# Matmuls of weight zero moved from every tile of keys to seven tiles around each change of heads

## The reference

```python
qh = (q @ Wq.T + bq).reshape(b, t, h, d).transpose(0, 2, 1, 3)
kh = (k @ Wk.T + bk).reshape(b, -1, h, d).transpose(0, 2, 1, 3)
attn = jax.nn.softmax(jnp.einsum('bhtd,bhsd->bhts', qh, kh) * scale, axis=-1)
out = jnp.einsum('bhts,bhsd->bhtd', attn, vh)
...
x = x + jnp.tanh(g_xattn[0]) * _L0_xattn_ref(_layernorm(x, axis=-1), ctx_1024, ctx_1024, ...)
x = x + jnp.tanh(g_ffn[0]) * _L0_ffn_ref(_layernorm(x, axis=-1), ...)
x = x + jnp.tanh(g_xattn[1]) * _L1_xattn_ref(ctx_1024, ctx_1024, _layernorm(x, axis=-1), mask_Bx1xSxS2_bf1, ...)
x = x + jnp.tanh(g_ffn[1]) * _L1_ffn_ref(_layernorm(x, axis=-1), ...)
```

## Time and profile before

| | |
|---|---|
| median of 3 runs | 2881.51 us (2869.57 to 2913.2) |
| the profiled execution: time, span, mean granted clock | 2875.57 us, 2873.5 us, 0.927 |
| PE busy | 2664.2 us, 93% |
| DVE busy | 2173.8 us, 76% |
| ACT busy | 1946.9 us, 68% |
| chain that ended last | PE 88%, of that L967 32%, L919 25%, L938 14%, L986 6% of the span |

### The profile page before, as it was taken

How to read it: one execution, slowest core, us unless ns; L and a number is a source line. 1 busy time by engine, 2 the same in 40 slices (tenths; PEclk the granted TensorE clock), 3 DMA queues, 4 the chain that set the end, 5 groups by cost and what they waited for, 6 DMA issues and landing times.

```text
span 2873.5 us, 63043 instructions
## 1 busy us (share of the span) xinstructions
PE 2664.2 (93%) x27154; PEld 1107.1 (39%) x27156; DVE 2173.8 (76%) x2210; ACT 1946.9 (68%) x3545; POOL 41.2 (1%) x28
## 2 busy tenths in 40 slices
PE   2489999999999999999693899999999999999989
PEld 1244344444444433344341344444444443444444
DVE  5478788888888877863533888888888887888334
ACT  1158778878888877786330288887888886888842
POOL 3000000000000000000001000000000000000000
PEclk8569899999999988999895699999999998999989
DMA  6210000000000000002201000000000000000010
GB/s 239 80 58 28 22 26 27 28 27 28 28 26 26 26 26 21 24 15 92 91 1 55 13 28 28 28 27 26 26 27 27 28 28 22 27 26 19 2 60 8
DMA packets 38657, 103.60 MB, mean 36 GB/s; under 512 B 4164, under 2 KB 14936, under 8 KB 38120
## 3 DMA queue, kind: packets, MB, share of 16 engines
q1 hardware_dynamic: 36936, 99.14, 9.4%
q10 hardware_dynamic: 1440, 0.40, 0.1%
HBM read 83.72 MB, written 15.80 MB: 35 GB/s over the span
## 4 chain that ended last, share of the span: by engine, by line
PE 88%; DVE 5%; DMA 3%; SPq 3%; ACT 1%; issue 1%; POOL 0%; ACTq 0%; DVEq 0%; POOLq 0%
PE ps L967 32%; PE ps L919 25%; PE ps L938 14%; PE ps L986 6%; PE ps L1065 3%; DVE m_part L650 3%; PE ps L1073 3%; SPq L290 2%; PE ps L879 1%; DMA q_parts<-probs 1%; SPq L299 1%; PE ps L909 1%; DMA probs<-in_mask_t 1%; DVE probs L606 1%; DMA k_parts<-probs 1%
## 5 line engine op out<-in xcount | busy, mean ns | idle before, releaser
L650 DVE TENSOR_REDUCE m_part<-ps 128x2 f32<-128x1024 f32 (+1 forms) x1664 | 1946.2, 1184 | 346.6 <-PE ps L938 239.8
L488 ACT ACTIVATE probs<-ps 128x512 f32<-128x512 f32 (+1 forms) x3264 | 1771.0, 595 | 482.7 <-PE ps L919 468.3
L967 PE MATMUL ps<-probs,v_all 128*9 128x256 f32 x13056 | 1033.5, 389 | 1.4 <-ACT o_raw L468 0.5
L919 PE MATMUL ps<-q_ring,k_ring 35*128 35x512 f32 x3264 | 852.0, 506 | 0.4
L938 PE MATMUL ps<-k_ring,q_ring 33*128 33x512 f32 (+1 forms) x3328 | 718.2, 425 | 90.4 <-DVE m_part L650 36.2
L919 PEld LDWEIGHTS ps<-q_ring,k_ring 35*128 35x128 f32 x3264 | 328.4, 186 | 554.9 <-ACT probs L488 500.2
L986 PE MATMUL ps<-neg_i,zeros 128*9 128x256 bf16 x6392 | 475.4, 277 | 0.0
L967 PEld LDWEIGHTS ps<-probs,v_all 128*9 128x9 f32 x13056 | 194.4, 88 | 564.4 <-ACT probs L488 455.2
L938 PEld LDWEIGHTS ps<-k_ring,q_ring 33*128 33x128 f32 x3328 | 336.6, 197 | 179.5 <-DVE m_part L650 104.6
L986 PEld LDWEIGHTS ps<-neg_i,zeros 128*9 128x9 bf16 x6392 | 175.1, 89 | 176.4 <-issue 14.3
L671 DVE RECIPROCAL r_den<-ps 128x8 f32<-128x8 f32 x32 | 6.6, 207 | 123.4 <-PE ps L946 123.4
(11 more groups left out here) (121 smaller groups left out, 601.2 us busy)
## 6 DMA issues: line engine op xcount, KB each, us to landing
k_ring<-k_parts SPq DMA_DIRECT2D x384, 96.0 KB
k_ring<-k_parts SPq DMA_DIRECT2D x128, 112.2 KB
k_ring<-gate_rows SPq DMA_DIRECT2D x16, 512.0 KB, 7.0
probs<-in_mask_t SPq DMA_DIRECT2D x10, 640.0 KB, 4.4
k_parts<-probs SPq DMA_DIRECT2D x12, 512.0 KB, 3.1
k_parts<-big SPq DMA_DIRECT2D x12, 512.0 KB, 3.1
q_ring<-q_parts SPq DMA_DIRECT2D x128, 32.0 KB
big<-in_w SPq DMA_DIRECT2D x1, 2048.0 KB, 11.3
```

What stands on the lines that cost most here:

```text
L488: A(probs[0:k, n % PSLOTS, HALF * half:HALF * half + HALF], ps[0:k, e_bank(unit), :], ACT.Exp, scale=SCALE).then_inc(sem(f"exp_done{l}"), 1)
L650: V.tensor_reduce(m_part[:, h % 2, :, p, c], mx(n % 2)[:, :, 0:chunk_w[c]], AX.X, ALU.max).then_inc(sem(f"mx_done{l}"), 1)
L919: pe.matmul(bank, k_ring[row:row + ROWS_EXP, koff:koff + P], q_ring[row:row + ROWS_EXP, qoff:qoff + HALF], start=not masked, stop=True).th ...
L967: mm = pe.matmul(ps[32 * g:32 * g + VW, 7, 0:QGW], v_all[0:k, t, h, :], probs[0:k, n % PSLOTS, QGW * g:QGW * g + QGW], start=(t == 0), sto ...
```

## The change

The loop that issues groups now issues three of them in a row after the weighing of tiles 0, 1, 2, 3, 47, 48 and 49 of a head (NT is 51), and none after any other tile. Weighing runs two steps behind, so these are steps 2 to 5 of a head, its steps 49 and 50, and step 0 of the next. Nothing else changes. Executed groups go from 50 a head to 21 (the last head of a layer: 49 to 18), recorded matmuls of L986 from 6392 to 2664. In the changed kernel's listing all PE lines are 4 higher.

```diff
@@ -60,6 +60,10 @@
 EB = 3
 LAG = 2
 WARM = 5
+
+
+DENSE = 3
+DENSE_AT = (0, 1, 2, 3, NT - 4, NT - 3, NT - 2)
 
 
 KCH = -(-TK // HALF)
@@ -1012,7 +1016,7 @@
                         n = h * NT + t - LAG
                         if n >= 0:
                             weigh(l, n // NT, n % NT)
-                            if n % NT < NT - 1:
+                            for _ in range(DENSE if n % NT in DENSE_AT else 0):
                                 keep_warm()
```

## The result

The changed kernel takes 2749.14 us (median of 3 runs, 2748.89 to 2751.86) against 2881.51 before: a ratio of 0.9563, 95% interval 0.9514 to 0.9612. Forecast was 2744 us. The profiled execution took 2751.86 us, its span is 2749.9 us. The spread of three runs went from 44 us to 3 us. In the changed kernel's listing the lines of PE are 4 higher than before: score L923, max L942, weigh L971, group L990.

The account below looks back on a forecast made before the run. PE was taken to set the pace in mid-head, partly at half clock. From 2875.6 us, 82 for fewer groups and 49 for the clock come off, giving 2744 us; own range 2727 to 2765, 2705 to 2800 for 0.8.

Parts of the forecast that it names:

- Part one: Saving from removed groups, net of added ones: 2.6 us a head over 30 heads, some 3 us from two last heads.
- the six falls: Six heads of the earlier profile partly at half clock, losing 48.8 us together; all six taken as gone.
- Its two terms: Per head: 43 middle tiles save 0.096 us each, 4.1 us; 14 added groups cost 0.107 each, 1.5 us.
- PE sets the pace there too, so I hide none of it: At the seven tiles with three groups, every added group costs its full 0.107 us, 1.5 us a head.
- my 1.33: Mean time in us from score to score in a head before the change, taken as 67.7/51.
- The score banks' loop: A score's first half to next tile's second half takes at least 1.24 us, making middle tiles 1.23, not 1.22.
- Part two: Clock gain at heads' ends: three groups where one stood keep the clock up, giving 49 us.
- the thin stretch at a head's end: PE's last work in a head, few rows: two max units, a 35-row score, a 4-row weighing; the clock falls behind it.
- my 131: Total forecast saving in us, the 82 from groups and the 49 from the clock.
- The middle falls: Rival: without groups the clock falls in the middle of heads, 880 us more, about 3620 us; chance 0.08.
- Another wait in place of the groups: Rival: another wait keeps middle tiles at 1.33 us, so 2872 us; chance 0.05.
- Falls that remain and last: Rival: three groups don't hold the clock at heads' ends; six falls cost 38 us each, 2972 us; chance 0.06.

Follow-up runs that it names:

- experiment 1: Changed kernel with one group put back after every other tile except a head's last, the three at the seven tiles kept: 2869.85 us, ratio 0.9979 to the kernel before.
- Experiment 6: Changed kernel with exponentials of 448 instead of 512 columns after each layer's first head: 2727.51 us, median of six; a head falls from 67.07 to 66.24 us.
- experiment 2: Changed kernel with three groups after each of a layer's first eight tiles and none later: 3817.77 us, ratio 1.3225 to the kernel before.
- experiment 3: Changed kernel with groups only after a layer's first eight tiles, and the 4-key tile weighed over 128 rows, padded with zeros: 2696.73 us, ratio 0.9343 to the kernel before.
- experiment 4: Changed kernel with groups reading 4 rows instead of 128 after a layer's first eight tiles: 4130.47 us, ratio 1.4308 to the kernel before.
- experiment 7: Kernel before, its groups unchanged, with the 4-key tile weighed over 128 rows, the other 124 against zeros: 2836.66 us.
- experiment 5: Changed kernel with one group instead of three at each of its seven tiles: 2976.8 us (2892.67 to 3082.58, 4 executions).

## Why the prediction was right

- **Part one, 82 us.** It came out as 75. From copy to copy, the 28 heads behind the first of each layer took 1009.4 and 986.2 us in layers 0 and 1 before, and 937.3 us in each after: 121.0 us less, of which the six falls are 48.8. The rest is 72.2 us, 2.58 a head, where I had 2.6. The two last heads gave 1.6 and 1.3 us, my 3. But I had counted 30 heads, and the first of each layer gave nothing: layer 0's ended at 266.6 us before and 266.9 after. At its start the clock was at half for 3.4 us before and 6.6 after, and in layer 1's, which started at 1.00 before, it was down for 10 us.
- **Its two terms.** Both were a little off and cancel. The 14 added groups cost 1.10 us, not 1.5. The term for them rests on "PE sets the pace there too, so I hide none of it", and this is wrong in two of the seven tiles (experiment 1). It also means that the 0.90 us of max matmuls in the earlier trace rows hold a wait for DVE, which I had ruled out as a bound: it binds in the one step with two max units. Middle tiles save 0.086 us, not 0.096. The 67.7 us behind my 1.33 stand in no row (the head has 69.67), and the scores of plain tiles before, at 403.97, 405.29 and 406.61 us, come every 1.32; after, they come every 1.23. And two tiles behind the transposes of the next head's maxima a score pair waits longer for ACT, which copies them (0.80 us for the pair, 0.64 in experiment 1). That takes 0.16 us a head back: 43 x 0.09 - 0.16 = 3.7 us.
- **The score banks' loop.** It had been hidden, and it came out as read from the last head: intervals of 1.21 and 1.24, a late second half every other time, 1.11 in the last head. Experiment 6 shows it as a cause: 0.83 us a head.
- **Part two, 49 us.** No head behind the first of a layer is below 1.00. That each fall was tied to the thin stretch at a head's end, and that 128 rows hold the clock, was argued from six falls; experiments 2, 3, 4 and 7 show it by changing rows alone. The size belongs to the execution that I started from. On the chip of experiment 7 the kernel before took 2920.76 us and that experiment, which takes away only the falls behind heads' ends, 2836.66: there they cost some 84 us.
- **Where the number owes to luck.** Between the two profiled executions the change gave 123.7 us, not 131. Between the medians it gave 132.4, which is nearly my 131, since the execution that I started from was 6 us under its median.
- **The rivals.** *The middle falls*: refuted here and in experiment 2: in layer 0 three heads without any group hold 1.00 to their ends, and the clock falls at the end of the last of them. *Another wait in place of the groups*: the loop took only 0.02 us of 0.11. *Falls that remain and last*: the change as made has none, but the danger was larger than I priced it. I gave a fall 38 us and let the next change end it; with one group (experiment 5) two falls last 208 and 338 us, and with none a layer stays down to its last head or through it.
- What stays open: the start of each layer's first head. In layer 0's the clock was down for 6.6 us in the changed kernel, 27 us in experiment 7 and 102 us in experiment 6. Weighings are few there, but no experiment aimed at it.

## What to carry to other kernels

Filler matmuls pay for the clock only where PE's real work is thin; find those places by cutting the trace at the program's own joints and reading the granted clock, for busy time did not show them here. Before adding filler, see whether the thin instruction itself can be widened: a contraction over 4 rows padded to 128 with values of zero took the same time and did the work of 21 groups a head. Before counting a price in every place, look for places where the engine already waits: two of seven hid it. And when work comes off the bounding engine, compute the next loop through the buffers: it was in the trace already, in the one head where that engine had less to do.

## What the runs showed of the hardware

- In these kernels the granted clock follows the rows that matmuls use, not the time that they fill. With 4 rows instead of 128 in groups of the same length and number, the attention ran at 0.50 instead of 1.00 from the end of each layer's first head on (4130 against 2749 us); with 128 rows instead of 4 in one weighing a head, at 1.00 instead of 0.50 from the fourth and the second change of heads on (2697 against 3818 us). PE read as busy in all of them. The edits change the rows of a matmul and of its weight load together, so which of the two counts is not shown.
- Work that holds the high clock need not restore it: in experiment 2 a head without groups stays at 1.00 if it starts there (65.36 us) and at 0.50 if it starts there (110.05 us).
- Matmuls with 9 columns of weights and 4 rows take the same time as with 9 columns and 128 rows (0.54 and 0.55 us for a weighing).
